# A vision tower on Trainium2: the patch embedding with its operands exchanged and computed one image further ahead

## The chip, the cores and the metric

The kernel runs on one core of one Trainium2 chip. The metric is the device time of one execution in microseconds (us), the median of several runs. Engines are called PE (TensorE matmul; PEld is its weight load), DVE (VectorE), ACT (ScalarE), POOL (GpSimd) and SP (SyncE, which only issues DMAs here). Everything is float32 unless said otherwise.

## The reference, cut to what matters

128 images of 3 x 224 x 224 are cut into 14 x 14 = 196 patches of 768 numbers. A patch embedding gives 256 features each, a class token goes in front (197 tokens), then come an attention block and a feed-forward block, each on a layernorm of the tokens and added to them.

```python
patches = x.reshape(B, C, gh, 16, gw, 16) ... .reshape(B, 196, 768)
h = einsum('bnp,dp->bnd', patches, W) + b            # W: 256 x 768
h = concatenate([cls_tok, h], axis=1)                 # B x 197 x 256
h = h + attention(layernorm(h))                       # 16 heads of 16, causal, low-rank projections, rms norm of q and k
h = h + coupled_ffn(layernorm(h))                     # three cycles of a small network and an update
```

## The kernel before, in words

The program has two passes. The first goes through the images one by one and ends with h1 = h + attention, stored to DRAM. The second reads h1 back and does the feed-forward part for two pairs of images at a time; neither the change nor any step of the prediction touches it.

Every engine runs its own instruction stream, written out by hand and tied together by semaphores. In the first pass each stream is a loop over steps n (`images`), from -1 to B + 2, and a step works on four images at once, so that each engine always finds work of some image:

- image n + 1: embedding, layernorm, transposition of the normed tokens, projection to q, k, v and r (a further product of the tokens, added to k);
- image n: rms norm of q and k, the weighting of k, the split of q and k into a high and a low part;
- image n - 1: transposes of k and q, scores with queries in rows, of which only the maxima are taken, and a transposition of these;
- image n - 2: scores with keys in rows (scoresT), their exponentials, the causal clearing, the product with v;
- image n - 3: the context is turned back to rows, divided, added to h (residual), and stored.

An image has 197 tokens, kept as a tile of 128 rows (t = 0) and one of 69 (t = 1). The lines that matter here:

**PE.** `tok` (L1008) computes the embedding of a tile t: for each of six slices k of the 768 inputs, the 128 (or 69) tokens of `xb` are the stationary operand (weights) and the 256 columns of `w_tok` move; a float32 product makes two weight loads and two matmuls, so twelve instructions a tile. Column 0 of `xb` is a zero column in the place of the class token. The six slices are issued in three parts of two (four instructions) per tile, between the transposes of k and q (`qk_transpose`, L1086) and the scoresT products (`products`, L1047). `tok` writes bank 6 for t = 0 and bank 7 for t = 1 (`W`). The step of PE in order: k transposes and q transposes with parts of the embedding between them, scoresT 0 to 3 with the last parts between them, scores 0 and 1 (L1111 to L1119), transpose of the normed tokens t = 0 (`hn_transpose`, L1023), product with v of the first half (`pv`, L1071 and L1075), transpose t = 1, pv of the second half, scores 2, projection (L1034) of t = 0, scores 3, projection of t = 1, transpose of the maxima (L1016), transposes of the context (`ctx_transpose`, L1094). Scores use banks in the order `SBANK`, the first two uses being banks 6 and 7, so they wait until DVE has read the embedding out of them (`h_ready`); the projection of t = 1 uses bank 7 too, and is read by ACT (`qkv_ready`).

**DVE.** `embed` (L758) adds bias and class token (`tok_add`) and puts the tile into `h`, of which there are four buffers: before image m overwrites its buffer, the residual of image m - 4 must be done on POOL (`h1_ready`). `stats` (L765, L767) takes mean and variance, `hn_apply` (L772) norms the tile. In DVE's step the order is: `rms_sum` (L784), `attend` (L825, L831), `rms_small` (L789 to L796; L791 squares rs, L794 multiplies by xh), `rms_mul` (L803, twice), embed and stats of tile 0, hn_apply 0, embed and stats of tile 1, `maxima` of scores 0 (L838 and L842 twice), hn_apply 1, maxima 1, `k_sum` 0 (L814, L816), maxima 2, `k_sum` 1, maxima 3, a copy of the transposed maxima (`mxT_copy`, L779).

**POOL.** In order: `residual` (L486) of both tiles, `k_weighted` (L468, L470) of tile 0, `norm` 0 (L446, and L448, which takes the reciprocal root by a power), `select` 0 and 1 (L454, L458: causal clearing of the exponentials), norm 1, select 2 and 3, k_weighted 1, `q_low_part` twice. pv of the second half waits for all four selects (`m_done`).

**ACT** copies k and q out of PSUM, takes the exponentials (L537, L541), copies the normed tokens, the context and q, k, v. **SP** per step: maxima rows to DRAM and back into qZ, store of h1, k and q into their zero-padded forms kZ and qZ (L340), and last the load of the patches of image n + 3 (L320), which waits until the embedding of image n + 1 has read that buffer.

A part of PE's step, as it stands before:

```python
embed_part(0, 0)                      # tok(x, xpar, 0, (0, 1))
qk_transpose(k2, KB, 2); qk_transpose(k2, KB, 3)
embed_part(0, 1)
qk_transpose(q2, QB, 0); qk_transpose(q2, QB, 1)
embed_part(0, 2)
```

Of the kernel before, what the change touches and what calls it, by code (L numbers as in the profile page):

```python
# [42 lines left out]
def build(nc, a, out):  # L43
# [17 lines left out]
    with ctx:  # L61
# [10 lines left out]
        tok_add = sb("tok_add", [P, 2, D])  # L72
# [43 lines left out]
        xb = sb("xb", [P, 2, KT, T])  # L116
# [78 lines left out]
        tok_done = sem("tok_done")  # L195
# [70 lines left out]
        def state(cyc):  # L266
# [7 lines left out]
            (tok_add[:, 0, :], a["tok_b"].partition_broadcast(P)),  # L274
            (tok_add[:, 1, :], a["tok_b"].partition_broadcast(P)),
# [18 lines left out]
        N_CV = 20  # L294
        N_W = 16 * (len(small_w) + 1)

        def images(eng, step):


            for n in range(-1, B + 3):  # L300
                step(n, n % 4)
# [11 lines left out]
        def _(sp):  # L313
            for dst, src in small_w:
                sp.dma_start(dst, src).then_inc(s_w, 16)
            sp.wait_ge(s_w, N_W - 16)
            sp.dma_start(tok_add[0:1, 0, :], a["cls"]).then_inc(s_w, 16)

            def load_x(m, par):
                sp.dma_start(xb[:, par, :, 1:T], a["x"][m]).then_inc(x_loaded[par], 16)  # L320
# [31 lines left out]
            def step(n, r):  # L352
# [14 lines left out]
                if there(n + 3):  # L367
                    sp.wait_ge(tok_done, n * 2 + 4)
                    load_x(n + 3, par)
# [45 lines left out]
        def _(pool):  # L415
# [73 lines left out]
            def step(n, r):  # L489
                if there(n - 3):  # L490
                    residual(n - 3, (r + 1) % 4)
                if there(n):
                    k_weighted(n, r, 0)
                if there(n + 1):
                    norm(n + 1, 0)
                if there(n - 2):
                    select(n - 2, 0)
                    select(n - 2, 1)
                if there(n + 1):
                    norm(n + 1, 1)  # L500
                if there(n - 2):
                    select(n - 2, 2)
                    select(n - 2, 3)
# [206 lines left out]
        def _(dve):  # L710
# [3 lines left out]
            v.memset(xb[:, :, :, 0:1], 0.0).then_inc(s_cv, 1)  # L714
# [13 lines left out]
            dve.wait_ge(s_w, N_W)  # L728
            v.tensor_scalar(wq_row[:], wq_row[:], float(HD) ** -0.5, None, ALU.mult).then_inc(s_cv, 1)
            dve.wait_ge(s_cv, 13)  # L730
# [21 lines left out]
            def embed(m, par, t):  # L752

                M = TS[t]
                dve.wait_ge(tok_done, m * 2 + t + 1)
                if later(m, 4):
                    dve.wait_ge(h1_ready, m * 2 + t - 7)
                v.tensor_tensor(h[:M, par, t, :], ps[:M, W[t], 0:D], tok_add[:M, t, :], ALU.add)\  # L758
                 .then_inc(h_ready, 1)
# [86 lines left out]
            def step(n, r):  # L846
# [4 lines left out]
                if there(n - 3):  # L851
                    attend(n - 3)
                if there(n):
                    rms_small(n)
                    rms_mul(n, r, 0)
                    rms_mul(n, r, 1)
                if there(n + 1):
                    embed(n + 1, xr, 0)
                    stats(n + 1, xr, 0)
                if there(n + 1):  # L860
                    hn_apply(n + 1, xr, 0)
                    embed(n + 1, xr, 1)
                    stats(n + 1, xr, 1)
                if there(n - 1):
                    maxima(n - 1, 0)
                if there(n + 1):
                    hn_apply(n + 1, xr, 1)
# [119 lines left out]
        def _(pe):  # L987
# [16 lines left out]
            def tok(m, par, t, ks):  # L1004

                M = TS[t]
                for k in ks:
                    mm = t_.matmul(ps[:M, W[t], 0:D], xb[:, par, k, t * P:t * P + M], w_tok[:, k, :],  # L1008
                                   start=k == 0, stop=k == KT - 1)
                if KT - 1 in ks:  # L1010
                    mm.then_inc(tok_done, 1)

# [84 lines left out]
            def scores(m, i):  # L1097

                for u in range(3):
                    use = 3 * i + u  # L1100
                    b = SBANK[use]
                    if use < 2 and there(m + 2):
                        pe.wait_ge(h_ready, m * 2 + 5 + use)
# [19 lines left out]
            def step(n, r):  # L1123
                m, o, x = n - 1, n - 2, n + 1
                xpar = 1 - r % 2

                def embed_part(t, part):
                    if there(x):
                        if part == 0:
                            if t == 0:  # L1130
# [261 lines left out]
```

## Time and profile before

| | |
|---|---|
| median of 3 runs | 4179.03 us (4177.65 to 4179.39) |
| the profiled execution's own time | 4180.67 us |
| its span, from the first to the last instruction | 4178.9 us |
| mean granted TensorE clock | 0.991 of full speed |
| first pass | up to about 2730 us of the span, 132 steps, the first and last ones with less in them |
| second pass | the rest |

The profile is of one execution on its one core. Busy times of PE overlap with its weight loads, and the duration of a matmul holds its way through the array, so the distance between starts says what one costs in a row of them. The chain of waits is followed back from the last instruction to what released each one. An instruction on DVE or ACT can start some 0.08 us before the one in front of it has ended.

### The profile page before, as it was taken

Reading aid. Unit: us, or ns where it says so; the run is one execution under the profiler, and the core shown is the slowest. Engines: PE = TensorE matmul, PEld = TensorE weight load, DVE = VectorE, ACT = ScalarE, POOL = GpSimd, SP = SyncE. Lnnn points to the kernel's source line nnn. Section 1 sums busy time; section 2 is a strip of 40 time slices with the busy share of each in tenths; the row PEclk is TensorE's granted clock in tenths of the full one; section 3 lists DMA queues with packets and bytes.
Section 4 is the critical chain, followed back from the end, with each engine's and each line's share of the span. In section 5 each row is a group of like instructions: output and inputs, shape, how many; then the busy total and the mean of one; then the engine's idle time right before and its main releaser. Section 6 shows DMA issues by size and latency. Waiting matters only on the chain.

```text
span 4178.9 us, 82357 instructions
## 1 busy us (share of the span) xinstructions
PE 3928.7 (94%) x29199; PEld 2687.5 (64%) x29454; DVE 3152.4 (75%) x7326; ACT 2484.6 (59%) x5890; POOL 1688.5 (40%) x2704
## 2 busy tenths in 40 slices
PE   6999999999999999999999999879999999999998
PEld 4777777777777777777777777644444444444444
DVE  6777777777777777777777777657776776777776
ACT  4666666666666666666666666534444444444443
POOL 3666666666666666666666666510000000000000
PEclk9999999999999999999999999989999999999999
DMA  3444444444444444444444444311111111211111
GB/s 94 120 120 120 120 119 120 119 120 120 120 119 121 121 120 119 119 119 119 119 119 119 119 119 119 98 53 51 57 60 47 59 58 47 62 56 50 61 53 39
DMA packets 281753, 398.34 MB, mean 95 GB/s; under 512 B 27777, under 2 KB 232066, under 8 KB 281346
## 3 DMA queue, kind: packets, MB, share of 16 engines
q1 hardware_dynamic: 281346, 393.07, 35.7%
q8 instruction: 237, 3.88, 0.4%
q14 instruction: 170, 1.39, 0.1%
HBM read 132.06 MB, written 53.26 MB: 44 GB/s over the span
## 4 chain that ended last, share of the span: by engine, by line
PE 62%; DVE 30%; issue 3%; another core or an unknown queue 2%; ACT 2%; DMA 1%; POOL 0%; SPq 0%; DVEq 0%; POOLq 0%
PE ps L1008 17%; PE ps L1270 13%; DVE mx L842 12%; PE ps L1086 7%; PE ps L1279 7%; DVE mx L838 7%; PE ps L1288 4%; DVE k L816 4%; PE ps L1284 3%; PE ps L1047 3%; PE ps L1094 3%; DVE k L814 2%; ACT a L663 1%; DVE st L765 1%
## 5 line engine op out<-in xcount | busy, mean ns | idle before, releaser
L1008 PE MATMUL ps<-w_tok,xb 128*128 128x256 f32 (+1 forms) x3072 | 835.4, 395 | 0.5 <-DVE small L750 0.3
L1270 PE MATMUL ps<-X,cn_w 128*128 128x394 f32 x1536 | 552.3, 502 | 0.0
L517 POOL TENSOR_SCALAR ve<-mv 128x4 f32<-128x4 f32 x64 | 14.8, 232 | 1287.5 <-DVE mv L891 1287.5
L537 ACT ACTIVATE p<-ps 128x394 f32<-128x394 f32 x1024 | 454.6, 499 | 127.1 <-PE ps L1047 127.1
L842 DVE TENSOR_REDUCE mx<-ps 69x2 f32<-69x396 f32 x1024 | 529.0, 556 | 0.0
L1008 PEld LDWEIGHTS ps<-w_tok,xb 128*128 128x128 f32 (+1 forms) x3072 | 450.7, 165 | 81.4 <-issue 1.6
L486 POOL TENSOR_TENSOR h<-h,att 128x256 f32<-128x256 f32 (+1 forms) x256 | 182.4, 732 | 662.4 <-DVE att L831 662.2
L655 ACT ACTIVATE a<-ps,cn_b 128x394 f32<-128x394 f32 x384 | 226.2, 589 | 368.0 <-PE ps L1270 354.1
L838 DVE TENSOR_REDUCE mx<-ps 128x4 f32<-128x512 f32 x512 | 351.0, 685 | 100.3 <-remote 100.1
L1047 PE MATMUL ps<-qZ,kT 128*128 128x396 f32 (+1 forms) x2048 | 396.9, 326 | 5.0 <-DMA qZ<-mx_scratch 4.8
L1118 PE MATMUL ps<-kZ,qT 128*69 128x396 f32 x1024 | 395.8, 453 | 0.3 <-DVE h L758 0.3
L1270 PEld LDWEIGHTS ps<-X,cn_w 128*128 128x128 f32 x1536 | 280.0, 191 | 176.1 <-issue 2.7
L454 POOL TENSOR_SCALAR_AFFINE_SELECT p<-p 128x512 f32<-128x512 f32 x512 | 345.2, 674 | 99.2 <-ACT p L537 98.8
L468 POOL TENSOR_TENSOR qkv<-qkv,wk_row 128x256 f32<-128x256 f32 (+1 forms) x256 | 295.0, 1152 | 218.9 <-DVE qkv L803 218.9
L555 ACT ACTIVATE sq<-ps 128x256 f32<-128x256 f32 (+1 forms) x512 | 196.0, 383 | 281.9 <-PE ps L1034 281.9
L1047 PEld LDWEIGHTS ps<-qZ,kT 128*128 128x128 f32 (+1 forms) x2048 | 314.8, 166 | 66.8 <-issue 6.3
L531 ACT ACTIVATE qT<-ps 128x396 fp32r<-128x396 f32 x512 | 228.1, 498 | 168.3 <-PE ps L1086 168.2
L1279 PE MATMUL ps<-a,cn_w 128*128 128x394 f32 x768 | 304.3, 518 | 10.7 <-DVE hk L945 6.6
L531 ACT ACTIVATE qkv<-ps 128x512 f32<-128x512 f32 (+1 forms) x512 | 306.6, 599 | 0.0
L926 DVE SCALAR_TENSOR_TENSOR u<-X,c_tf,th 128x394 f32<-128x394 f32 x192 | 119.7, 623 | 225.2 <-ACT th L667 225.2
L1034 PE MATMUL ps<-w_qkv,hnT 64*128 64x256 f32 (+1 forms) x2048 | 286.2, 399 | 0.0
L1071 PE MATMUL ps<-p,qkv 128*17 128x197 f32 x4096 | 254.0, 334 | 30.4 <-POOL p L458 29.5
(137 smaller groups left out, 8419.4 us busy)
## 6 DMA issues: line engine op xcount, KB each, us to landing
kZ<-kT SPq DMA_DIRECT2D x512, 198.0 KB, 3.4
qZ<-qT SPq DMA_DIRECT2D x256, 396.0 KB, 4.8
xb<-in_x SPq DMA_DIRECT2D x128, 588.0 KB, 6.9
h_scratch<-h SPq DMA_DIRECT2D x128, 128.0 KB
hl<-h_scratch SPq DMA_DIRECT2D x64, 256.0 KB
hk<-h_scratch SPq DMA_DIRECT2D x64, 256.0 KB
out<-hk SPq DMA_DIRECT2D x64, 256.0 KB
h_scratch<-h SPq DMA_DIRECT2D x128, 69.0 KB
```

The source lines that it names most:

```text
L454: g.affine_select(out=v, in_=v, compare_op=ALU.is_ge, fill=0.0, base=0, pattern=[[0, HG], [1, P]], channel_multiplier=-1).then_inc(m_done, 1)
L468: g.tensor_tensor(k, k, wk, ALU.mult).then_inc(kw_done, 1)
L531: return s.activation(o, i_, ACT.Copy)
L537: s.activation(p0[:, i, 2 * jj:2 * jj + 2, :], ps[:, (b0, b1)[jj], 0:2 * TE].rearrange("p (a b) -> p a b", b=TE)[:, :, 0:T], ACT.Exp).then ...
L838: v.tensor_reduce(mx[:, 0, 4 * i:4 * i + 4], ps[:, b0, :].rearrange("p (a b) -> p a b", b=P), AX.X, ALU.max, negate=True).then_inc(s_max, 1)
L842: v.tensor_reduce(mx[:T1, 1, 4 * i + 2 * jj:4 * i + 2 * jj + 2], ps[:T1, b, 0:2 * TE].rearrange("p (a b) -> p a b", b=TE), AX.X, ALU.max, ...
L1008: mm = t_.matmul(ps[:M, W[t], 0:D], xb[:, par, k, t * P:t * P + M], w_tok[:, k, :], start=k == 0, stop=k == KT - 1)
L1047: mm = t_.matmul(ps[:M, b, x_ * 2 * N:x_ * 2 * N + 2 * N].rearrange("p (a b) -> p a b", b=N), kT[:, par, j, keys], qZ[:, :, j, queries], s ...
L1086: mm = t_.transpose(ps[:, banks[b], j2 * TE + t * P:j2 * TE + t * P + M].bitcast(F32R), x2[:M, t, h:h + 2, :, :].rearrange("p h s d -> p ( ...
L1118: t_.matmul(bank, qT[:, j, P:T], kZ[:, :, j, :], start=True, stop=False)
L1270: mm = t_.matmul(ps[:, 4 * c + mt, 0:N2], cn_w1[:, f, mt * P:mt * P + P], X[:, c, state(cyc), f, :], start=f == 0, stop=f == FT - 1)
L1279: mm = t_.matmul(ps[:, 4 * c + 2, 0:N2], cn_w2[:, f, :], a1[:, c, f, :], start=f == 0, stop=f == 1)
```

## The change

What it does, engine by engine:

- **PE.** `tok` now has a 128 x 128 block of `w_tok` (slice k, feature tile ft) as the stationary operand, and the 196 patches of an image move. Its result has features in rows and patches in columns, bank 6 for ft = 0 and bank 7 for ft = 1. Twelve instructions per feature tile as before. It works on image n + 2 instead of n + 1 and waits for `h_ready` before the second feature tile; the loops of all engines start at n = -2. At the head of each step, four transposes (`h_transpose`) bring image n + 1 back to tokens in rows, all into bank 7, after ACT has read that bank.
- **DVE.** `embed_copy` adds the bias (one per row now) and puts a feature tile into `hT`, columns 1 to 196; column 0 holds the class token from the start. `embed` becomes a plain copy out of bank 7 into h. Both embeds move to directly behind `attend`, both stats behind `rms_small`, ahead of `rms_mul`; then come hn_apply 0, embed_copy 0, hn_apply 1, embed_copy 1, and the maxima.
- **POOL.** Both norms come directly behind the residual, ahead of k_weighted 0; the four selects follow one another.
- **SP.** The patches are loaded for image n + 4; the buffer has no column for the class token. `tok_add` (two broadcast loads and one late load of a row) gives way to two small loads, `tok_bT` and `clsT`.

```diff
@@ -291,13 +295,13 @@
             (gc_b3[:, 0:1], a["gc_b3"].partition_broadcast(P)),
             (ar[:], a["ar"].partition_broadcast(P)),
         ]
-        N_CV = 20
-        N_W = 16 * (len(small_w) + 1)
+        N_CV = 21
+        N_W = 16 * len(small_w)
         def images(eng, step):
-            for n in range(-1, B + 3):
+            for n in range(-2, B + 3):
                 step(n, n % 4)
         def there(m):
...
@@ -313,11 +317,9 @@
         def _(sp):
             for dst, src in small_w:
                 sp.dma_start(dst, src).then_inc(s_w, 16)
-            sp.wait_ge(s_w, N_W - 16)
-            sp.dma_start(tok_add[0:1, 0, :], a["cls"]).then_inc(s_w, 16)
             def load_x(m, par):
-                sp.dma_start(xb[:, par, :, 1:T], a["x"][m]).then_inc(x_loaded[par], 16)
+                sp.dma_start(xb[:, par, :, :], a["x"][m]).then_inc(x_loaded[par], 16)
             def store_h1(m, par):
                 sp.wait_ge(h1_ready, m * 2 + 1)
...
@@ -364,9 +366,9 @@
                     else:
                         sp.wait_ge(qT_ready, n * 4)
                     pad(qZ, qT, slice(0, H // 2), qZ_loaded)
-                if there(n + 3):
-                    sp.wait_ge(tok_done, n * 2 + 4)
-                    load_x(n + 3, par)
+                if there(n + 4) and n >= -2:
+                    sp.wait_ge(tok_done, n * 2 + 6)
+                    load_x(n + 4, r % 2)
             images(sp, step)
             for par in range(2):
...
@@ -489,18 +491,14 @@
             def step(n, r):
                 if there(n - 3):
                     residual(n - 3, (r + 1) % 4)
+                if there(n + 1):
+                    norm(n + 1, 0)
+                    norm(n + 1, 1)
                 if there(n):
                     k_weighted(n, r, 0)
-                if there(n + 1):
-                    norm(n + 1, 0)
                 if there(n - 2):
-                    select(n - 2, 0)
-                    select(n - 2, 1)
-                if there(n + 1):
-                    norm(n + 1, 1)
-                if there(n - 2):
-                    select(n - 2, 2)
-                    select(n - 2, 3)
+                    for i in range(4):
+                        select(n - 2, i)
                 if there(n):
                     k_weighted(n, r, 1)
                     q_low_part(n, r, 0)
...
@@ -711,7 +709,6 @@
             v = nc.vector
             v.memset(w_qkv[:], 0.0).then_inc(s_cv, 1)
             v.memset(qkv[:], 0.0).then_inc(s_cv, 1)
-            v.memset(xb[:, :, :, 0:1], 0.0).then_inc(s_cv, 1)
             v.memset(qZ[:].bitcast(F32), 0.0).then_inc(s_cv, 1)
             v.memset(kZ[:].bitcast(F32), 0.0).then_inc(s_cv, 1)
             v.memset(q2[:].bitcast(F32), 0.0).then_inc(s_cv, 1)
...
@@ -726,8 +723,10 @@
             v.memset(qkv[:, :, :, V, :, HD:HD + 1].rearrange("p a t h o -> p (a t) h o"), 1.0).then_inc(s_cv, 1)
             dve.wait_ge(s_w, N_W)
+            for b in range(2):
+                v.tensor_copy(hT[:, b, :, 0], clsT[:]).then_inc(s_cv, 1)
             v.tensor_scalar(wq_row[:], wq_row[:], float(HD) ** -0.5, None, ALU.mult).then_inc(s_cv, 1)
-            dve.wait_ge(s_cv, 13)
+            dve.wait_ge(s_cv, 14)
             v.tensor_tensor(wk_row[:], wk_row[:], wq_row[:], ALU.mult).then_inc(s_cv, 1)
             dve.wait_ge(s_cp, 10)
             v.memset(mv2[:], 1.0).then_inc(s_cv, 1)
...
@@ -752,11 +751,17 @@
             def embed(m, par, t):
                 M = TS[t]
-                dve.wait_ge(tok_done, m * 2 + t + 1)
+                dve.wait_ge(h_transposed, m * 2 + 2)
                 if later(m, 4):
                     dve.wait_ge(h1_ready, m * 2 + t - 7)
-                v.tensor_tensor(h[:M, par, t, :], ps[:M, W[t], 0:D], tok_add[:M, t, :], ALU.add)\
-                 .then_inc(h_ready, 1)
+                v.tensor_copy(h[:M, par, t, :], ps[:M, W[1], t * D:t * D + D]).then_inc(h_ready, 1)
+
+            def embed_copy(m, buf, ft):
+                dve.wait_ge(tok_done, m * 2 + ft + 1)
+                if m >= 2:
+                    dve.wait_ge(h_transposed, m * 2 - 2)
+                v.tensor_scalar(hT[:, buf, ft, 1:T], ps[:, W[ft], 0:NP], tok_bT[:, ft:ft + 1], None,
+                                ALU.add).then_inc(hT_ready, 1)
             def stats(m, par, t):
                 M = TS[t]
...
@@ -850,21 +855,27 @@
                     rms_sum(n, 1)
                 if there(n - 3):
                     attend(n - 3)
+                if there(n + 1):
+                    embed(n + 1, xr, 0)
+                    embed(n + 1, xr, 1)
                 if there(n):
                     rms_small(n)
+                if there(n + 1):
+                    stats(n + 1, xr, 0)
+                    stats(n + 1, xr, 1)
+                if there(n):
                     rms_mul(n, r, 0)
                     rms_mul(n, r, 1)
                 if there(n + 1):
-                    embed(n + 1, xr, 0)
-                    stats(n + 1, xr, 0)
+                    hn_apply(n + 1, xr, 0)
+                if there(n + 2):
+                    embed_copy(n + 2, r % 2, 0)
                 if there(n + 1):
-                    hn_apply(n + 1, xr, 0)
-                    embed(n + 1, xr, 1)
-                    stats(n + 1, xr, 1)
+                    hn_apply(n + 1, xr, 1)
+                if there(n + 2):
+                    embed_copy(n + 2, r % 2, 1)
                 if there(n - 1):
                     maxima(n - 1, 0)
-                if there(n + 1):
-                    hn_apply(n + 1, xr, 1)
                 if there(n - 1):
                     maxima(n - 1, 1)
                 if there(n):
...
@@ -1001,14 +1012,22 @@
             pe.wait_ge(s_pwc, 5)
             pe.wait_ge(s_cp, 10)
-            def tok(m, par, t, ks):
-
-                M = TS[t]
+            def tok(m, par, ft, ks):
+
                 for k in ks:
-                    mm = t_.matmul(ps[:M, W[t], 0:D], xb[:, par, k, t * P:t * P + M], w_tok[:, k, :],
+                    mm = t_.matmul(ps[:, W[ft], 0:NP], w_tok[:, k, ft * P:ft * P + P], xb[:, par, k, :],
                                    start=k == 0, stop=k == KT - 1)
                 if KT - 1 in ks:
                     mm.then_inc(tok_done, 1)
+
+            def h_transpose(m, buf):
+                pe.wait_ge(hT_ready, m * 2 + 2)
+                for t in range(2):
+                    M = TS[t]
+                    for ft in range(FT):
+                        mm = t_.transpose(ps[:M, W[1], t * D + ft * P:t * D + ft * P + P],
+                                          hT[:, buf, ft, t * P:t * P + M], ident[:, :])
+                    mm.then_inc(h_transposed, 1)
             def mx_transpose(m):
                 for t in range(2):
...
@@ -1099,8 +1118,10 @@
                 for u in range(3):
                     use = 3 * i + u
                     b = SBANK[use]
-                    if use < 2 and there(m + 2):
-                        pe.wait_ge(h_ready, m * 2 + 5 + use)
+                    if use < 2 and there(m + 3):
+                        pe.wait_ge(hT_ready, m * 2 + 7 + use)
+                    elif use == 1 and there(m + 2):
+                        pe.wait_ge(h_ready, m * 2 + 6)
                     elif 2 <= use < 6 and there(m - 1):
                         pe.wait_ge(e_done, m * 12 + use - 7)
                     elif use >= 6:
...
@@ -1121,18 +1142,23 @@
             def step(n, r):
-                m, o, x = n - 1, n - 2, n + 1
-                xpar = 1 - r % 2
-
-                def embed_part(t, part):
-                    if there(x):
-                        if part == 0:
-                            if t == 0:
-                                pe.wait_ge(x_loaded[xpar], x * 8 + 16 - 8 * xpar)
+                m, o, x, y = n - 1, n - 2, n + 1, n + 2
+                ypar = r % 2
+
+                def embed_part(ft, part):
+                    if there(y):
+                        if part == 0 and ft == 0:
+                            pe.wait_ge(x_loaded[ypar], y * 8 + 16 - 8 * ypar)
                             if there(n):
-                                pe.wait_ge(qkv_ready, n * 4 + 2 + t)
-                        tok(x, xpar, t, (2 * part, 2 * part + 1))
-
+                                pe.wait_ge(qkv_ready, n * 4 + 2)
+                        elif part == 0 and there(x):
+                            pe.wait_ge(h_ready, x * 2 + 2)
+                        tok(y, ypar, ft, (2 * part, 2 * part + 1))
+
+                if there(x):
+                    if there(n):
+                        pe.wait_ge(qkv_ready, n * 4 + 3)
+                    h_transpose(x, 1 - r % 2)
                 if there(m):
                     pe.wait_ge(k2_ready, n * 2)
                     qk_transpose(k2, KB, 0)
...
@@ -1192,16 +1218,12 @@
                 if there(o):
                     if there(m):
                         pe.wait_ge(s_max, n * 12 - 11)
-                    elif there(x):
-                        pe.wait_ge(h_ready, x * 2 + 1)
                     pv(o, (r + 2) % 4, 0)
                 if there(x):
                     hn_transpose(x, 1)
                 if there(o):
                     if there(m):
                         pe.wait_ge(s_max, n * 12 - 10)
-                    elif there(x):
-                        pe.wait_ge(h_ready, x * 2 + 2)
                     pv(o, (r + 2) % 4, 1)
                 if there(m):
                     pe.wait_ge(kZ_loaded[1], n * 32)
...
@@ -1209,6 +1231,8 @@
                 if there(x):
                     if isinstance(n, int) and n == -1:
                         pe.wait_ge(s_blk, 128)
+                    if there(y) and not there(m):
+                        pe.wait_ge(hT_ready, y * 2 + 2)
                     pe.wait_ge(hnT_ready, x * 2 + 1)
                     if there(o):
                         pe.wait_ge(ctx0_ready, n - 1)
```

## Rows read from the trace of the kernel before

**Rows 1.** The page, part 1: busy us, share of the span, instructions.
```profile
PE 3928.7 (94%) x29199; PEld 2687.5 (64%) x29454; DVE 3152.4 (75%) x7326; ACT 2484.6 (59%) x5890; POOL 1688.5 (40%) x2704
```

**Rows 2.** Chain of waits, one step: start us, us, what.
```profile
1507.22 0.34 PE ps L1016 x2
1507.56 0.88 PE ps L1094 x8
...
1509.03 0.96 PE ps L1008 x4
...
1513.72 0.91 PE ps L1008 x4
...
1515.13 0.86 PE ps L1008 x4
...
1516.51 0.88 PE ps L1008 x4
...
1518.96 0.69 DVE mx L838
...
1523.63 0.33 another core or an unknown queue
...
1528.03 0.34 PE ps L1016 x2
```

**Rows 3.** Timeline of PE, same step, scores 0 and second context product.
```profile
1518.25 0.44 PE L1111 MATMUL ps<-kZ,qT 128*128 128x256 f32 x2
...
1521.60 0.34 PE L1023 MATMUL ps<-ident,hn 69*128 69x69 f32 x2
1522.17 0.53 PE L1071 MATMUL ps<-p,qkv 128*17 128x197 f32 x8 [0.23 <-POOL p L458]
```

**Rows 4.** Timeline of PE: an early step's start.
```profile
71.91 0.34 PE L1016 MATMUL ps<-ident,mx 128*16 128x128 f32 x2 [1.35 <-DVE mx L842]
```

**Rows 5.** Timeline of PE: the first step without embedding.
```profile
2672.28 0.34 PE L1016 MATMUL ps<-ident,mx 128*16 128x128 f32 x2 [0.37 <-DVE mx L842]
...
2682.18 0.77 PE L1111 MATMUL ps<-kZ,qT 128*128 128x256 f32 x2 [0.48 <-DMA kZ<-kT]
```

**Rows 6.** Timeline of DVE, same step: start us, us, instruction, count, [idle before <-releaser].
```profile
1507.60 0.35 DVE L779 CAST mxT<-ps 16x197 fp32r<-16x197 f32 x1 [0.43 <-PE ps L1016]
...
1510.55 0.79 DVE L791 TENSOR_TENSOR y<-rs 128x64 f32<-128x64 f32 x1
1511.45 0.22 DVE L794 TENSOR_TENSOR y<-y,xh 128x64 f32<-128x64 f32 x1
...
1511.96 1.29 DVE L803 TENSOR_TENSOR qkv<-qkv,rms 128x512 f32<-128x512 f32 x2
...
1513.62 0.43 DVE L765 BATCH_NORM_STATS2 st<-h 128x6 f32<-128x256 f32 x1
...
1517.41 0.42 DVE L758 TENSOR_TENSOR h<-ps,tok_add 69x256 f32<-69x256 f32 x1 [1.50 <-PE ps L1008]
...
1520.52 0.40 DVE L772 TENSOR_SCALAR hn<-h,mv,rstd 69x256 f32<-69x256 f32 x1
```

**Rows 7.** Timeline of POOL, same step.
```profile
1509.83 1.43 POOL L486 TENSOR_TENSOR h<-h,att 128x256 f32<-128x256 f32 x2 [5.12 <-DVE att L831]
1512.84 0.97 POOL L468 TENSOR_TENSOR qkv<-qkv,wk_row 128x256 f32<-128x256 f32 x1 [1.57 <-DVE qkv L803]
...
1514.58 0.22 POOL L446 TENSOR_SCALAR ve<-mv 128x1 f32<-128x1 f32 x1
1514.89 0.57 POOL L448 TENSOR_TENSOR rstd<-ve,power 128x1 f32<-128x1 f32 x1
...
1519.64 0.64 POOL L454 TENSOR_SCALAR_AFFINE_SELECT p<-p 128x512 f32<-128x512 f32 x1
...
1520.65 0.78 POOL L454 TENSOR_SCALAR_AFFINE_SELECT p<-p 128x512 f32<-128x512 f32 x1
1521.39 0.64 POOL L458 TENSOR_SCALAR_AFFINE_SELECT p<-p 69x276 f32<-69x276 f32 x1
```

More of the change, by code:

```diff
@@ L71, in build @@
         w_tok = sb("w_tok", [P, KT, D])
-        tok_add = sb("tok_add", [P, 2, D])
+        tok_bT = sb("tok_bT", [P, FT])
+        clsT = sb("clsT", [P, FT])
         w_qkv = sb("w_qkv", [P, 4, 8, HD])
@@ L113, in build @@
         c_base = sb("c_base", [P, 1])
-        xb = sb("xb", [P, 2, KT, T])
+        xb = sb("xb", [P, 2, KT, NP])
+        hT = sb("hT", [P, 2, FT, T])
         h = sb("h", [P, 4, 2, D])
@@ L194, in build @@
         h1_stored = [sem("h1_stored0"), sem("h1_stored1")]
-        tok_done = sem("tok_done")
+        tok_done = sem("tokT_done")
+        hT_ready = sem("hT_ready")
+        h_transposed = sem("h_transposed")
         h_ready = sem("h_ready")
@@ L273, in build @@
             (w_tok[:], a["w_tok"]),
-            (tok_add[:, 0, :], a["tok_b"].partition_broadcast(P)),
-            (tok_add[:, 1, :], a["tok_b"].partition_broadcast(P)),
+            (tok_bT[:], a["tok_bT"]),
+            (clsT[:], a["clsT"]),
             (wk_row[:], a["wk"].partition_broadcast(P)),
@@ L1366 @@
         "x": patches.transpose(0, 2, 1, 3),
-        "cls": np.asarray(inputs["cls_tok"]).reshape(1, D),
+        "clsT": np.asarray(inputs["cls_tok"]).reshape(-1, P).T,
         "w_tok": w.T.reshape(KT, P, D).transpose(1, 0, 2),
-        "tok_b": lay("tok_b"),
+        "tok_bT": lay("tok_b").reshape(-1, P).T,
         "wdq": lay("attn_W_DQ"), "wuqT": lay("attn_W_UQ").T,
```

## The prediction

> **What bounds the kernel now.** The page comes first: PE is busy for 94% of the span [rows 1]. A share says nothing of which engine ends a wait, so the chain of waits of one step in mid-run comes next [rows 2]. The step from one transpose of the maxima (L1016) at 1507.22 to the next at 1528.03 takes 20.81 us. The first half of the chain is all PE: context transposes, q/k transposes, and the embedding in six pieces of four instructions. Then DVE embeds rows 128 to 196, reduces the maxima of scores 0 and 1, and waits once more, before the maxima of scores 2. The same step in the timelines shows what stands behind these waits. PE starts scores 0 at 1518.25, and DVE's maxima follow 0.71 later. PE's second context product (L1071) starts at 1522.17 after waiting for POOL's causal clearing; scores 2 stand behind it, and DVE waits for those [rows 2, 3]. So two legs count: PE's from the start of the step to scores 0, and the one to the second context product, which PE and POOL reach almost together. The step repeats: 2672.28 minus 71.91 is 2600.37, or 125 steps of 20.80 us [rows 4, 5]. Below, +x is x us after the step's start at 1507.22.
>
> **PE, embedding.** Removed: the six pieces 0.96 x 3 + 0.91 + 0.86 + 0.88 = 5.53 us (three of the 0.96 kind, one shown) [rows 2]. The cheapest has 0.86 / 4 = 0.215 per instruction of 256 moving columns, its weight loads hidden. The first load of a piece behind transposes lies open: 0.96 - 0.86 = 0.10 for 128 columns of weights, 0.91 - 0.86 = 0.05 for 69. Added: 24 instructions again, with 196 columns; by proportion 0.215 x 196 / 256 = 0.165 each, since a load of 0.10 still fits behind 0.165. The bounds: no cheaper than 0.165, no dearer than 0.165 + 0.10 = 0.265, every load open. I take 0.165, as all rows of this line are like that. Four pieces cost 4 x 0.165 + 0.10 = 0.76, the two behind the score products 0.66 and 0.68: 4.38 in all. The four transposes are of the shapes of the context transposes, eight of which take 0.88 [rows 2]: 4 x 0.11 = 0.44. Net 4.38 + 0.44 - 5.53 = -0.71 us per step, on the chain. Scores 0 start at +11.03 - 0.71 = +10.32, DVE's maxima at +11.03.
>
> Four waits move with this. PE's h_transpose waits for ACT's third copy of qkv, ahead of everything else in the step; the context transposes keep PE until +1.2, and I cost it at nothing (a later copy would cost what it is late). The new wait on h_ready before the second feature tile stands at about +6, embed is over by +4.5. The patches are still loaded two steps ahead; that DMA issue stays last in SP's step, so nothing queues behind it. The padded keys become the next limit: in the first step without embedding PE started scores 0 at 2682.18, +9.90, after waiting for that DMA [rows 5]. As +10.32 is later, this cover holds with 0.4 to spare.
>
> **DVE, front of the step.** Added: two copies of 196 columns out of PSUM; the nearest row is the copy of 197 columns, 0.35 [rows 6]. The two plain copies into h cost at most what the additions cost, 0.42. embed and stats move ahead of the weighting of q and k, and with them comes a wait that was covered: embed(n+1) overwrites the h that residual(n-3) reads, and POOL ends that residual at 1509.83 + 1.43 = +4.04 [rows 7]. So DVE stands still between attend and the second embed, and everything behind it on DVE with it.
> What is given back: y (L791) takes 0.79 there, and its sister of the same shape 0.22 [rows 6]; it starts at 1510.55 with POOL's residual running and ends at 1511.34, 0.08 after it. Behind embed it would meet an idle POOL. The Trainium skill, "SBUF — State Buffer", section "SBUF: two separate sides", states the rule: a VectorE instruction with two SBUF inputs and a GpSimd one that reads SBUF exclude each other for a whole instruction. This trace agrees; if it did not hold, y would stay 0.79 long and all that follows would come 0.57 later.
> The sum: second embed +4.08, rms_small from +4.43, whose y now ends at about +4.8, stats from +5.3. From the first statistics to the end of rstd POOL and DVE take 1514.89 + 0.57 - 1513.62 = 1.84 [rows 6, 7], so rstd 0 is there at +7.14; rstd 1, one ve and rstd later (0.88, from 1514.58), at +8.0. The weighting of q and k ends at +7.9 instead of 1511.96 + 1.29 = +6.03. hn_apply twice and both copies follow; the last waits for PE's second feature tile until +9.5 and ends at +9.9, before scores 0 start (+10.32) and scores 1 want its bank. So 1.2 us of DVE work (embed, stats, hn_apply of the second tile) leave the stretch between the last embedding product and the end of maxima 1, and only 0.40 (the hn_apply at 1520.52 [rows 6]) stood where it counted.
>
> **POOL.** k_weighted(0) now stands behind both norms, and is what they delay: start +8.0 instead of 1512.84, that is +5.62. It takes 1514.58 - 1512.84 = 1.74, so select 0 starts at +9.7. A clean pair of selects takes 1520.65 - 1519.64 = 1.01, the last 1521.39 + 0.64 - 1520.65 = 1.38 [rows 7]: 9.7 + 3 x 1.01 + 1.38 = +14.15, against 1522.03, or +14.81. PE starts 0.14 later: +14.3. PE itself is there at +13.9: the transposes at 1521.60 end 0.22 later [rows 3], less 0.71. The old start was +14.95. The second context product moves by 0.65 if POOL's durations stay, and by up to 1.05 if they shrink (its 1.74 holds a part in which it met DVE's weighting). Scores 2, maxima 2, k_sum(1), maxima 3 follow unchanged. DVE is free for maxima 2 in time: maxima 0 at +11.03, maxima 1 and k_sum(0) without the 0.40.
>
> So the step gets shorter by 0.65 to 1.05; I take 0.80, as PE's 0.71 is firm and part of the wait at 1522.17 should go. 125 x 0.80 = 100 us. The **ends**: one step more in front (an embedding alone, a few us, partly given back by earlier statistics), and the last embedding step is emptied: together +1, an estimate. The profiled execution took 4180.67 (span 4178.9); 4180.67 - 99 = 4082. The median of the three runs, 4179.03, lies 1.6 lower: **4080 us**. The second pass is untouched. A measurement tells apart about 0.2%, 8 us.
>
> **Rivals.**
> (a) *The transposed chain is late.* POOL's selects end later than reckoned, since DVE's front is longer or POOL meets hn_apply and the weighting of q and k: the wait at 1522.17 stays while PE arrives sooner. For: that leg now crosses between POOL and DVE four times (residual, embed, norms, k_weighted). Against: no row shows rstd delaying anybody. With half of it lost, 0.3 a step: 4179 - 37 = 4142. At 0.65 lost nothing would be gained at all: 4180.
> (b) *The whole gain.* PE is the only bound, 1.05 a step or more: 4179 - 131 = 4048.
> (c) *Slower: weight loads lie open.* A stream of 196 columns no longer covers the next load of 128 columns. Place: the 24 embedding instructions. Price: 24 x 0.265 + 0.44 - 5.53 = +1.27 a step, 4179 + 159 = 4338. It decides from 0.03 per instruction on (24 x 0.03 = 0.71). Against: 0.10 is well below 0.165, and pieces of 256 columns show no open load but the first. The Trainium skill speaks for it: "TensorE: Matmul & The Clock Gate", Part 3, says that weight loads overlap running matmuls only in other row groups; loads of all 128 rows are hidden here, in the 0.86 piece, so the trace disagrees.
> (d) *The change doesn't bind.* The padded keys or the copies hold scores 0 where they are: 4180.
>
> **Chances.** Forecast (0.65 to 1.0 a step) 0.57; (a) 0.23, a quarter of it within 0.2%; (b) 0.10; (c), or another loss like it, 0.07; (d) 0.03. Faster: 0.57 + 0.10 + 0.17 = 0.84 and some of the rest, 0.85; same 0.07; slower 0.08. The range takes in (b) and most of (a): 4040 to 4148.
>
> **What would show it.** Right: pieces of the embedding at 0.66 to 0.76; four transposes in 0.44; the step at 20.0; y at 0.22; the wait before L1071 gone or as it was. Wrong: pieces near 1.06 (c); a wait for POOL before L1071 above 0.3 (a); PE waiting for DVE before scores 1, or for a DMA before scores 0 (d); half the clock in mid-run.

## The result and the profile after: slightly slower

The changed kernel takes **4195.15 us** (median of 6 runs, 4189.37 to 4197.29) against 4179.21 for the kernel before (6 runs, 4177.42 to 4185.15): ratio 1.0034, interval 1.0024 to 1.0044. The forecast was 4080 us, in a range of 4040 to 4148. The profiled execution took 4197.29 us, span 4195.5.

The page, part 1 and two groups of part 5 (busy, mean ns of one, idle before and its releaser):

```profile
PE 3856.1 (92%) x29711; PEld 2759.5 (66%) x29966; DVE 3143.9 (75%) x7583; ACT 2482.5 (59%) x5890; POOL 1709.7 (41%) x2704
...
L1018 PE MATMUL ps<-xb,w_tok 128*128 128x196 f32 x3072 | 697.2, 351 | 0.3 <-DVE small L749 0.3
...
L1090 PE MATMUL ps<-p,qkv 128*17 128x197 f32 x4096 | 252.2, 332 | 119.3 <-POOL p L460 117.9
```

PE is 73 us less busy than before [rows 1]: the work did get cheaper. But L1090, the context product, now waits 118 us for POOL's causal clearing.

The chain of waits, one step from its start at 1511.86 to the next at 1532.86, 21.00 us:

```profile
1511.86 0.34 PE ps L1035 x2
...
1513.07 0.44 PE ps L1028 x4
...
1514.12 0.76 PE ps L1018 x4
...
1519.50 0.71 PE ps L1018 x4
...
1520.70 0.72 PE ps L1018 x4
...
1527.12 1.68 another core or an unknown queue
...
1532.86 0.34 PE ps L1035 x2
```

The PE front is the forecast one: pieces of 0.76, 0.71 and 0.72 against 0.96 to 0.86 [rows 2], and 0.44 for the four transposes. What the chain gained there it lost in one wait of 1.68 ahead of maxima 2, where 0.33 stood [rows 2]. Three timelines of the same step show what it waits for. POOL (start us, us, instruction, [idle before]):

```profile
1518.40 1.14 POOL L450 TENSOR_TENSOR rstd<-ve,power 128x1 f32<-128x1 f32 x1
1519.87 0.59 POOL L450 TENSOR_TENSOR rstd<-ve,power 69x1 f32<-69x1 f32 x1
1520.43 0.68 POOL L470 TENSOR_TENSOR qkv<-qkv,wk_row 128x256 f32<-128x256 f32 x1
...
1521.89 0.64 POOL L456 TENSOR_SCALAR_AFFINE_SELECT p<-p 128x512 f32<-128x512 f32 x1
...
1524.94 0.82 POOL L456 TENSOR_SCALAR_AFFINE_SELECT p<-p 128x512 f32<-128x512 f32 x1
1525.72 1.13 POOL L460 TENSOR_SCALAR_AFFINE_SELECT p<-p 69x276 f32<-69x276 f32 x1
```

DVE:

```profile
1515.30 0.42 DVE L757 COPY h<-ps 128x256 f32<-128x256 f32 x1 [0.30 <-POOL h L488]
1515.99 0.42 DVE L757 COPY h<-ps 69x256 f32<-69x256 f32 x1 [0.26 <-POOL h L488]
1516.43 0.21 DVE L796 TENSOR_TENSOR y<-rs 128x64 f32<-128x64 f32 x1
1517.15 0.42 DVE L770 BATCH_NORM_STATS2 st<-h 128x6 f32<-128x256 f32 x1
...
1518.44 1.26 DVE L808 TENSOR_TENSOR qkv<-qkv,rms 128x512 f32<-128x512 f32 x2
...
1520.49 0.77 DVE L777 TENSOR_SCALAR hn<-h,mv,rstd 69x256 f32<-69x256 f32 x1
...
1526.12 0.41 DVE L819 CAST k<-qkv 128x512 fp32r<-128x512 f32 x1
```

PE, with the first transpose of the maxima and the one that follows the last embedding step:

```profile
69.18 0.34 PE L1035 MATMUL ps<-ident,mx 128*16 128x128 f32 x2 [1.34 <-DVE mx L847]
...
1527.00 0.53 PE L1090 MATMUL ps<-p,qkv 128*17 128x197 f32 x8 [1.01 <-POOL p L460]
...
2685.12 0.34 PE L1035 MATMUL ps<-ident,mx 128*16 128x128 f32 x2 [0.35 <-DVE mx L847]
```

Below, +x is x us after the step's start; a causal clearing is one pair of L456 and L460, and a duration is called clean when it is the shortest that the traces show for that instruction (0.64 or 0.65 and 0.46 for the pair). POOL's first rstd takes 1.14 beside DVE's weighting of q and k (L808), where it took 0.57 [rows 7]. The last causal clearing (L456, L460) takes 1526.85 - 1524.94 = 1.91, where it took 1.38 [rows 7], with DVE's cast of k beside it, and ends at +14.99. PE's second context product starts at +15.14, after a wait of 1.01; before it was +14.95 [rows 3]. A usual step grew by the same 0.19 (21.00 against 20.81). A few steps of the changed kernel are shorter (about 20.3), and the mean is (2685.12 - 69.18) / 125 = 20.93 against 20.80. That is 16 us in 125 steps, the whole difference of the medians. The ends nearly cancel: the front is 2.7 shorter (69.18 against 71.91), the rest behind the last of these transposes 3.8 longer (4195.5 - 2685.12 = 1510.4 against 4178.9 - 2672.28 = 1506.6).

### The profile page after: what moved, and what is told of

It is laid out like the page before. It is cut to its first block, busy times and chain, and to the rows that moved or that the text cites. A ratio compares the mean times of both kernels' runs of the same rounds, so it can differ in the third digit from the quotient of the medians.

```text
span 4195.5 us, 84016 instructions
## 1 busy us (share of the span) xinstructions
PE 3856.1 (92%) x29711; PEld 2759.5 (66%) x29966; DVE 3143.9 (75%) x7583; ACT 2482.5 (59%) x5890; POOL 1709.7 (41%) x2704
## 4 chain that ended last, share of the span: by engine, by line
PE 59%; DVE 26%; another core or an unknown queue 8%; issue 3%; ACT 2%; POOL 1%; DMA 1%; SPq 0%; DVEq 0%; POOLq 0%
PE ps L1018 13%; PE ps L1294 13%; DVE mx L847 11%; PE ps L1303 7%; PE ps L1105 7%; DVE mx L843 7%; PE ps L1312 4%; PE ps L1308 3%; PE ps L1066 3%; DVE k L821 3%; PE ps L1113 3%; DVE k L819 2%; ACT a L661 1%; PE ps L1325 1%
## 5 line engine op out<-in xcount | busy, mean ns | idle before, releaser
L1018 PE MATMUL ps<-xb,w_tok 128*128 128x196 f32 x3072 | 697.2, 351 | 0.3 <-DVE small L749 0.3
L1018 PEld LDWEIGHTS ps<-xb,w_tok 128*128 128x128 f32 x3072 | 487.7, 190 | 0.4 <-issue 0.4
L1066 PE MATMUL ps<-qZ,kT 128*128 128x396 f32 (+1 forms) x2048 | 378.7, 317 | 6.0 <-DMA qZ<-mx_scratch 5.5
L1090 PE MATMUL ps<-p,qkv 128*17 128x197 f32 x4096 | 252.2, 332 | 119.3 <-POOL p L460 117.9
L456 POOL TENSOR_SCALAR_AFFINE_SELECT p<-p 128x512 f32<-128x512 f32 x512 | 352.1, 688 | 7.8 <-ACT p L535 7.8
L460 POOL TENSOR_SCALAR_AFFINE_SELECT p<-p 69x276 f32<-69x276 f32 x512 | 312.8, 611 | 0.0
```

Source lines behind the costliest of these rows:

```text
L456: g.affine_select(out=v, in_=v, compare_op=ALU.is_ge, fill=0.0, base=0, pattern=[[0, HG], [1, P]], channel_multiplier=-1).then_inc(m_done, 1)
L460: g.affine_select(out=v, in_=v, compare_op=ALU.is_ge, fill=0.0, base=0, pattern=[[0, HG], [1, T1]], channel_multiplier=-1).then_inc(m_done, 1)
L1018: mm = t_.matmul(ps[:, W[ft], 0:NP], w_tok[:, k, ft * P:ft * P + P], xb[:, par, k, :], start=k == 0, stop=k == KT - 1)
L1066: mm = t_.matmul(ps[:M, b, x_ * 2 * N:x_ * 2 * N + 2 * N].rearrange("p (a b) -> p a b", b=N), kT[:, par, j, keys], qZ[:, :, j, queries], s ...
```

## The experiments

The theories: **A**, POOL's chain from the residual to the last clearing is lengthened because the new order puts DVE's weighting beside rstd and DVE's cast of k beside the last clearing. Its rivals are that only one of the two matters, that the wait of embed for the residual (0.30 + 0.26 in the rows above) is what costs, or that ACT lengthens the clearing (**C**). Steps below are the mean of 125, from the first and the 126th transpose of the maxima in each trace.

### e1_order: weighting ahead of embed and stats

```
 DVE:  attend(n - 3)
-      embed x2; rms_small(n); stats x2
-      rms_mul(n)
+      rms_small(n); rms_mul(n)
+      embed x2; stats x2
 POOL: residual(n - 3)
-      norm(n + 1) x2; k_weighted(n, 0)
+      k_weighted(n, 0); norm(n + 1) x2
```

> The changed kernel with one order put back: DVE weights q and k (rms_small, rms_mul) before it embeds and takes the statistics, and POOL weights k of tile 0 before both norms. The transposed embedding stays as it is. Theory A (POOL's last causal select is late, because k_weighted(0) stands behind the norms and because that makes it meet DVE's cast of k): k_weighted(0) starts 2.9 us earlier in the step, the last select ends before the cast, about 1.3 us earlier, PE's wait before the second context product falls from 1.0 to under 0.3, the step from 20.95 to about 20.0, the time to about 4075. Theory B (the embedding turned round is itself what costs: transposes, copies, the wait for the residual): the step stays at 20.9 and the time at 4190 to 4200.

Measured: 4137.65 us, ratio 0.9897 (0.9882 to 0.9911), step (2626.66 - 70.47) / 125 = 20.45. Timelines of PE, POOL and DVE in e1_order, a step that starts at 1501.50:

```profile
1508.25 0.93 PE L1015 MATMUL ps<-xb,w_tok 128*128 128x196 f32 x4 [0.41 <-DVE h L757]
...
1507.45 0.74 DVE L757 COPY h<-ps 128x256 f32<-128x256 f32 x2
...
1516.76 0.85 DVE L821 TENSOR_TENSOR k<-qkv,k 128x256 fp32r<-128x256 f32 x1
...
1509.36 0.57 POOL L450 TENSOR_TENSOR rstd<-ve,power 128x1 f32<-128x1 f32 x1
...
1514.53 0.46 POOL L460 TENSOR_SCALAR_AFFINE_SELECT p<-p 69x276 f32<-69x276 f32 x1
...
1515.89 1.44 POOL L472 TENSOR_TENSOR qkv<-qkv 69x256 f32<-69x256 f32 x1
```

rstd is back at 0.57 and the last clearing ends at +13.49, so both lengthenings come from the order. The time was still 63 us above the 4075 expected: the copies into h come at +5.95, so the embedding waits 0.41 for them, and DVE's L821 (0.55 in the changed kernel) now takes 0.85 beside POOL's L472 of the rows above. Part of the loss had moved to other places.

### e2_ksum_late: the cast of k behind maxima 2

```
       maxima(n - 1, 1)
-      k_sum(n, r, 0)
       maxima(n - 1, 2)
+      k_sum(n, r, 0)
       k_sum(n, r, 1)
```

> The changed kernel with DVE's k_sum(0) moved behind the maxima of scores 2, so that its cast cannot run while POOL clears. Theory A: the last select's second instruction falls from 1.2 us to 0.64 or less and PE's second context product starts about 0.5 earlier in the step; DVE now has 0.9 more to do behind the maxima of scores 2, so the step itself gets longer by 0.2 to 0.5 and the time is 4215 to 4260. Theory C (the last select is slow because ACT copies q at that time): the select stays at 1.2.

Measured: 4196.04 us (one run), step (2686.09 - 66.72) / 125 = 20.95. Timelines of PE and POOL in e2_ksum_late:

```profile
1532.94 0.34 PE L1034 MATMUL ps<-ident,mx 128*16 128x128 f32 x2 [1.14 <-DVE mx L847]
...
1547.23 0.53 PE L1089 MATMUL ps<-p,qkv 128*17 128x197 f32 x8 [0.19 <-POOL p L460]
...
1546.02 0.65 POOL L456 TENSOR_SCALAR_AFFINE_SELECT p<-p 128x512 f32<-128x512 f32 x1
1546.63 0.46 POOL L460 TENSOR_SCALAR_AFFINE_SELECT p<-p 69x276 f32<-69x276 f32 x1
```

With the cast away the last clearing is clean: it takes 1.07, ends at 1547.09, or +14.15, and the product starts at +14.29. The time stays where it was because two k_sum now follow maxima 2 on DVE: PE waits 1.14 for the last maxima instead of 0.35. It came out below the 4215 expected, as this new wait costs only what the other gave back. ACT's copies of q stayed where they were, so the clean clearing speaks against C too.

### e3_khigh_act: the cast of k on ACT

```
 ACT:  hnT_copy(n + 1, 0)
+      k_high_part(n, r, 0)
       q_high_part(n, r, 0); q_high_part(n, r, 1)
       ...; ctx_copy(n - 2, 1)
+      k_high_part(n, r, 1)
 DVE:  in k_sum
-      v.tensor_copy(k2[:M, t, :, 0:2, :], k4).then_inc(k_high, 1)
       dve.wait_ge(k_high, ...)
```

> The changed kernel with the cast of k (k_high) given to ACT, where the same copy of q already is: DVE keeps the subtraction only. Theory A: with no cast on DVE the last select takes 0.65 instead of 1.2, the second context product starts 0.5 earlier, and DVE is 0.45 shorter behind the maxima of scores 2: step 20.0 to 20.2, time 4080 to 4110. Theory C (ACT's copies slow POOL): the last select stays as long or gets longer, and only DVE's 0.45 are saved: step 20.5, time 4140.

Measured: 4085.59 us, ratio 0.9778 (0.9762 to 0.9794), step (2573.58 - 69.58) / 125 = 20.03. Timelines of PE and POOL in e3_khigh_act:

```profile
1470.55 0.34 PE L1042 MATMUL ps<-ident,mx 128*16 128x128 f32 x2 [0.22 <-DVE mx L854]
...
1484.84 0.53 PE L1097 MATMUL ps<-p,qkv 128*17 128x197 f32 x8 [0.17 <-POOL p L460]
...
1484.23 0.46 POOL L460 TENSOR_SCALAR_AFFINE_SELECT p<-p 69x276 f32<-69x276 f32 x1
```

The clearing is clean again (0.46), the product starts at +14.29, and DVE has less to do. As A expected.

### e4_qhigh_late: ACT's copies of q away from the clearing

```
 ACT:  hnT_copy(n + 1, 0)
-      q_high_part(n, r, 0); q_high_part(n, r, 1)
       ctx_copy(n - 2, 0); ...; ctx_copy(n - 2, 1)
+      q_high_part(n, r, 0); q_high_part(n, r, 1)
```

> The changed kernel with ACT's two copies of q moved behind the second context copy, away from POOL's last selects. Theory C (ACT's copies slow POOL): the last select's two instructions fall from 0.82 and 1.2 to 0.64 and 0.46, the second context product starts 0.9 earlier, time about 4090. Theory A: the first of them may fall a little, the second still meets DVE's cast and stays above 0.9; time 4170 to 4200.

Measured: 4219.49 us (one run), step (2710.03 - 69.13) / 125 = 21.13. Timeline of POOL in e4_qhigh_late:

```profile
1544.98 1.34 POOL L478 TENSOR_TENSOR q<-qkv,q 128x256 fp32r<-128x256 f32 x2 [0.89 <-ACT q L529]
...
1561.75 0.82 POOL L456 TENSOR_SCALAR_AFFINE_SELECT p<-p 128x512 f32<-128x512 f32 x1
1562.54 1.12 POOL L460 TENSOR_SCALAR_AFFINE_SELECT p<-p 69x276 f32<-69x276 f32 x1
```

0.82 and 1.12 stay as in the changed kernel (0.82 and 1.13), although ACT's copies of q now start at 1565.37, behind the end of the clearing at 1563.66. So C falls. The kernel itself was slower than expected, since POOL now waits for ACT's q (0.89).

### e7_five and e11_five_wait: five buffers of h, without and with the old wait

e7_five (e11_five_wait is the same with the last line kept at m * 2 + t - 7):

```
-h = sb("h", [P, 4, 2, D])
+h = sb("h", [P, 5, 2, D])      # index m % 5 at each use
-if later(m, 4): dve.wait_ge(h1_ready, m * 2 + t - 7)
+if later(m, 5): dve.wait_ge(h1_ready, m * 2 + t - 9)
```

> The changed kernel with five buffers of h instead of four, so that the embedding of image n+1 no longer waits for the residual of image n-3 in the same step. Theory A (DVE's and POOL's front pushes the last select into DVE's cast of k): the copies into h start 0.4 to 0.5 earlier, the statistics about 0.6, k_weighted(0) 0.5; the last select then ends before the cast starts at +14.3 and takes 1.1 instead of 1.8, the second context product starts a full 1 us earlier, the step is 20.0 to 20.2, the time 4085 to 4110: a wait of half a microsecond is worth nearly a whole one. Theory B (what is early on DVE is given back elsewhere, since L796 meets POOL's residual again): no more than 0.2 of a step, 4170 to 4195.

> e7 with the wait put back: five buffers of h, but the embedding still waits for the residual of image n-3, as if there were four. Everything else is e7. Theory A (that wait, and nothing of the buffers' place in memory or of the order, made e7 fast): back to the changed kernel, step 20.95, time 4190 to 4200, last select 1.8 again. Otherwise it stays near 4071.

Measured: e7_five 4070.87 us, ratio 0.9744 (0.9728 to 0.9761), step (2562.23 - 68.58) / 125 = 19.95. e11_five_wait 4191.13 us, ratio 1.0034 (1.0022 to 1.0047), step 20.94, the changed kernel's time. Timelines of PE, DVE and POOL in e7_five, a usual step of 19.91:

```profile
1485.89 0.34 PE L1035 MATMUL ps<-ident,mx 128*16 128x128 f32 x2 [0.35 <-DVE mx L847]
...
1499.94 0.53 PE L1090 MATMUL ps<-p,qkv 128*17 128x197 f32 x8
...
1488.96 0.74 DVE L757 COPY h<-ps 128x256 f32<-128x256 f32 x2
...
1500.14 0.44 DVE L819 CAST k<-qkv 128x512 fp32r<-128x512 f32 x1
...
1491.86 1.13 POOL L450 TENSOR_TENSOR rstd<-ve,power 128x1 f32<-128x1 f32 x1
...
1498.39 0.65 POOL L456 TENSOR_SCALAR_AFFINE_SELECT p<-p 128x512 f32<-128x512 f32 x1
1499.00 0.64 POOL L460 TENSOR_SCALAR_AFFINE_SELECT p<-p 69x276 f32<-69x276 f32 x1
```

rstd is as long as before the edit (1.13), yet the wait for the residual is gone and POOL's rstd starts 0.57 earlier, at +5.97. The last clearing ends at 1499.64, or +13.75, 0.50 ahead of the cast, and takes 1.25 instead of 1.91. So 0.66 more is saved on POOL. The product starts at +14.05 without a wait, 1.09 earlier than in the changed kernel, and the step is shorter by the same 1.09. A wait of 0.30 + 0.26 is worth 70 us in 125 steps by itself; it cost 4191.13 - 4070.87 = 120, because it pushed the clearing into the cast. Without it the time is 9 us below the forecast of 4080, with rstd as long as ever: the long rstd alone is not enough for the loss. No run takes the long rstd away and leaves all else, so what it costs by itself is not shown.

### e12_before_five and e9_before_khigh: the same two edits without the change

Both are the kernel before, with e7's buffers and e3's cast.

> The kernel before with five buffers of h. There the embedding comes 2 us after the residual has ended, so the wait costs nothing. Theory A: no difference, 4175 to 4183. If a fifth buffer were good in itself, it would be faster here too.

> The kernel before the change with only the cast of k given to ACT. It tells what of e3's gain has nothing to do with the embedding. Behind the maxima of scores 2 DVE is 0.45 shorter per step: 20.35, time 4120 to 4130, if the cast was merely work; with the cast also in POOL's way before the change (its k_weighted of tile 1 takes 1.35 there, but nobody waits for that) no more than this. If the turned embedding is worth nothing by itself, this kernel is as fast as e3, 4085.

Measured: e12_before_five 4179.42 us, ratio 1.0004 (0.9995 to 1.0013): nothing, as no wait for the residual stood there. e9_before_khigh 4138.03, ratio 0.9904 (0.9889 to 0.9918): the cast on ACT saves 41 us without the change, where the 4120 to 4130 expected asked for 50 to 60. On top of it the change saves 4138.03 - 4085.59 = 52. Timeline of POOL in e9_before_khigh, the last clearing:

```profile
1518.73 0.77 POOL L454 TENSOR_SCALAR_AFFINE_SELECT p<-p 128x512 f32<-128x512 f32 x1
1519.47 0.46 POOL L458 TENSOR_SCALAR_AFFINE_SELECT p<-p 69x276 f32<-69x276 f32 x1
```

It takes 1.20, where the kernel before has 1.38 [rows 7]. The second half is clean without the cast (0.46 against 0.64); the first half, beside DVE's hn_apply in both, stays at 0.77.

### e10_front and e6_front_khigh: embed stays in front, the weighting ahead of stats

e10_front (e6_front_khigh adds e3's edit):

```
 DVE:  attend(n - 3); embed x2; rms_small(n)
-      stats x2; rms_mul(n)
+      rms_mul(n); stats x2
 POOL: k_weighted(n, 0) ahead of the norms, as in e1_order
```

> The changed kernel with DVE's weighting of q and k ahead of the statistics and k_weighted(0) ahead of the norms on POOL; the copies into h stay right behind attend. Compared with e1, where PE waited 0.5 for the copies into h. Theory A: rstd of tile 0 falls from 1.1 to 0.6 as no weighting runs beside it, k_weighted(0) starts at about +6.3, the last select ends near +13.8, PE does not wait for h before the second feature tile: step 20.1, time 4090 to 4110. If the order of norms does not matter the time is that of the changed kernel, 4190 to 4200.

> e10 and e3 together: k_weighted(0) before the norms and the cast of k on ACT. Theory A: the selects end 0.3 before those of e3, so PE alone sets the second context product (+13.9): step 19.7 to 19.9, time 4040 to 4065. If PE's stretch from the step's start was already the bound in e3, the time is that of e3, 4085.

Measured: e10_front 4126.33 us, ratio 0.9876 (0.9862 to 0.9891), step 20.37; e6_front_khigh 4110.51, ratio 0.9838 (0.9824 to 0.9853), step 20.24. Both missed what was expected, and e6_front_khigh is slower than e3_khigh_act alone. Timelines of PE, DVE and POOL in e10_front:

```profile
1507.08 0.40 PE L1137 MATMUL ps<-kZ,qT 128*69 128x396 f32 x1 [0.48 <-DVE hT L763]
...
1505.56 1.14 DVE L777 TENSOR_SCALAR hn<-h,mv,rstd 69x256 f32<-69x256 f32 x1
1506.62 0.40 DVE L763 TENSOR_SCALAR hT<-ps,tok_bT 128x196 f32<-128x196 f32 x1
...
1504.08 0.57 POOL L450 TENSOR_TENSOR rstd<-ve,power 128x1 f32<-128x1 f32 x1
...
1505.49 0.64 POOL L456 TENSOR_SCALAR_AFFINE_SELECT p<-p 128x512 f32<-128x512 f32 x1
```

rstd is 0.57, but the norms now end just ahead of the selects, and DVE's second hn_apply takes 1.14 beside the first of them. The last copy of the transposed tokens comes behind it, and PE waits 0.48 for it before scores 1. That is the wait which the step of 20.37 kept.

### e8_five_khigh: both edits on the change

> Five buffers of h (e7) and the cast of k on ACT (e3) together, the version that should beat both kernels. Theory A: the second context product is set by PE alone in e7 already (DVE waits 1 us or less for scores 2), so only what DVE does behind the maxima of scores 2 can shrink, and there PE's scores 3 come next: e3 shows 2.22 from maxima 2 to maxima 3 against 2.35 in e7. Step 19.8, time 4050 to 4062. If the cast's 0.45 counted in full: step 19.5, 4015.

Measured: **4054.64 us** (5 runs, 4052.05 to 4060.75), ratio 0.9706 (0.9693 to 0.9719), step (2546.13 - 69.80) / 125 = 19.81, as expected. It beats both kernels. Chain of waits in e8_five_khigh, the end of a step:

```profile
1474.39 0.25 PE ps L1141
...
1474.66 0.53 DVE mx L850
...
1475.27 1.04 DVE mx L854 x2
...
1476.36 0.34 PE ps L1042 x2
```

From the step's start to 1474.64 the chain stays on PE; DVE stands in it only with the last maxima. PE is the bound that the prediction took it for.

| | kernel before | with the change |
|---|---|---|
| as it is | 4179 | 4195 |
| five buffers of h | 4179 | 4071 |
| cast of k on ACT | 4138 | 4086 |
| both | not run | 4055 |

## Why the prediction was wrong

**PE: right.** 0.76 for four pieces, then 0.71 and 0.72 (0.66 and 0.68 forecast), 4.47 in all against 4.38; transposes 0.44. Rival (c) is out: with every load open a piece would have taken 1.06.

**DVE's front: right in place.** The second copy into h starts at +4.13 (+4.08 forecast); its wait for the residual was foreseen (0.30 and 0.26). y takes 0.21 and stats start at +5.29, as forecast. The four waits at no cost held, in the whole run: the embedding (L1018) idles 0.3 us, scores 0 and 2 (L1132) 2.5 for the padded keys, the four transposes (L1028) not at all.

**The POOL paragraph failed**, by 0.84 of a step. Its sum, against the step shown:

- start of k_weighted(0): +8.0 forecast, +8.57 measured, **+0.57**. The step that failed is "from the first statistics to the end of rstd POOL and DVE take 1.84": the rows behind it were taken where DVE's weighting had ended. The same stretch took 2.39 here (1517.15 to 1519.54). In the new order the weighting starts at 1518.44, just behind the statistics, and rstd takes 1.14. e1_order and e10_front, which weight earlier, show 0.57.
- its length: 1.74 forecast, 1.46 measured (1520.43 to 1521.89), -0.28, the part that the text had said might shrink.
- three clean pairs of selects: 3.03 forecast, 3.05 measured, +0.02.
- last pair: 1.38 forecast, 1.91 measured, **+0.53**. A duration was carried over whose neighbours had moved. The old 1.38 was not clean: e9_before_khigh shows that 0.18 of it came with the cast. In the new order hn_apply is away from it, but maxima 1 starts 0.91 earlier (+12.71 against +13.62), the cast behind it comes at +14.26 instead of +15.18, and the clearing was still running. The prediction's own times say as much: with maxima 1 earlier by its 0.71 + 0.40, the cast starts at about +14.07, ahead of the clearing's forecast end. e2_ksum_late and e3_khigh_act, without that neighbour, show a clean 1.07.

The sum is 0.84: an end at +14.99 instead of +14.15. PE is free for the second context product at +14.13 and waits until +15.14, so its shorter front gains nothing, and the step is 0.13 longer in the mean. That e2_ksum_late and e3_khigh_act end the clearing at +14.15 and +14.14, the forecast time, is luck: their clearings start 0.3 late, as in the changed kernel, and the clean last pair gives 0.31 back.

**The sharing rule was used at one place only.** The rows show 0.57 against 1.14 for the same rstd, by what runs beside it. The Trainium skill, "SBUF — State Buffer", section "Who interferes with whom", has the rule for it: the pair of ports that VectorE and GpSimd share is an exclusive lock, and the one that issues second waits for the whole instruction. The prediction used this to free y, and did not ask which instructions the new order puts side by side. The rstd agrees with the rule in its length: the 0.57 that it grows by is about one of the two weighting instructions (1.26 for both). By recorded starts neither of the two agrees in its order. The rstd starts at 1518.40, 0.04 ahead of the weighting, the last select at 1525.72, 0.40 ahead of the cast, and both are the ones that get longer. The rule speaks of issue, and no view here shows when an instruction was issued.

**Rivals.** (a) named the place, the wait for POOL, and the crossing of the two engines. Its price was wrong: it took "nothing gained" as its worst, as if POOL's durations could only fall. "No row shows rstd delaying anybody" was not so, though off the chain: in the kernel before, DVE's first hn_apply (1515.50) stood idle for 1.12 until rstd was done. It was beside the point too, as here rstd is the one delayed. (b)'s 1.05 a step was not to be had by POOL alone: with no wait left, e7_five saves 20.80 - 19.95 = 0.85 in the mean and 0.90 in a usual step, as PE itself gets to the second context product at +14.05 and not +13.9. The prediction left the slower side to (c) "or another loss like it"; a wait on a leg that crosses engines four times should have carried it by name.

## What to carry to other kernels

Before durations of a trace are added up for a new order, lay the two engines that lengthen each other's instructions (here DVE and POOL) side by side in that order: a duration belongs to its neighbours, and work that comes *earlier* can collide too. A short wait ahead of such a leg is not worth its own length: 0.56 us of it cost 0.96 a step here, and the cure was one more buffer, worth nothing before the change. When a reorder has cleared one collision, look at once for the wait it hands to the next in-order engine, as e1_order and e10_front did.

## What the runs showed of the hardware

- An instruction with one tensor input met the same fate as those with two: DVE's hn_apply of 69 rows takes 0.40 [rows 6], 0.77 beside POOL's k_weighted (1520.49 above) and 1.14 beside a select (e10_front). Here the longer one is also the second by recorded start: k_weighted starts 0.06 ahead of it (1520.43), the select 0.07 (1505.49 against 1505.56).
- The last clearing is lengthened although it starts, and its first half even ends, ahead of the cast's recorded start: L456 takes 0.82 and ends at 1525.76, the cast starts at 1526.12. With the cast later or on ACT it takes 0.65 or less (e2_ksum_late, e3_khigh_act), so it is the cast that does it, but what decides the order of the two isn't settled. In e7_five L460 still takes 0.64 instead of 0.46, with 0.50 between its end and the cast's start, and in the kernel before 0.64 with 0.37 between them; e8_five_khigh and e9_before_khigh, without the cast, show 0.46.
- A column of 128 values through POOL's power takes 0.57, and beside DVE's weighting 1.14: very little work can be held up by as much as it takes.
